# Cross-attention and feed-forward kernel on one core: the rounding of the last batch's main probabilities on ScalarE, and one part of a layer norm one slot later on POOL

## What is computed

```python
    x = x + _L0_xattn_ref(_layernorm(x), ctx_1024, ctx_1024, mask, w_q, w_k, w_v, w_o)
    x = x + _L0_ffn_ref(_layernorm(x), kernel, bias, a, b)
```

## Time and profile before

| what | value |
|---|---|
| runs of the kernel | 519.60, 517.91, 517.69 us; median 517.91 |
| the profiled execution | 519.61 us, its span 517.8 us |
| busy share of the span | PE 87%, DVE 80%, POOL 76%, ACT 63% |
| chain that ended last | PE 45%, DVE 28%, ACT 14%, POOL 6% |
| mean granted clock of TensorE | 0.96 of full speed |

### The profile page before, as it was taken

How to read it: one execution, slowest core, us unless ns; L and a number is a source line. 1 busy time by engine, 2 the same in 40 slices (tenths; PEclk the granted TensorE clock), 3 DMA queues, 4 the chain that set the end, 5 groups by cost and what they waited for, 6 DMA issues and landing times.

```text
span 517.8 us, 15453 instructions
## 1 busy us (share of the span) xinstructions
PE 448.1 (87%) x5855; PEld 328.1 (63%) x5855; DVE 412.6 (80%) x1122; ACT 324.6 (63%) x837; POOL 393.3 (76%) x652
## 2 busy tenths in 40 slices
PE   3219768999999999999999999999999999888873
PEld 0116246667866686677766786668666866666652
DVE  4955756888899897978898888989897978887662
ACT  4905446577667776677667766777677766665621
POOL 3356158798978897788879888889788887899941
PEclk9658979999999999999999999999999999999898
DMA  8320139767796699679967797669868886679950
GB/s 308 120 61 11 30 58 202 130 128 152 169 175 130 128 199 154 114 122 176 173 130 137 161 167 149 132 133 192 161 122 146 141 159 128 134 128 182 165 122 26
DMA packets 218817, 71.91 MB, mean 139 GB/s; under 512 B 202785, under 2 KB 216882, under 8 KB 218738
## 3 DMA queue, kind: packets, MB, share of 16 engines
q1 hardware_dynamic: 217680, 69.25, 69.6%
q0 software_dynamic: 480, 1.31, 1.1%
q10 hardware_dynamic: 578, 0.30, 0.2%
HBM read 14.71 MB, written 4.19 MB: 37 GB/s over the span
## 4 chain that ended last, share of the span: by engine, by line
PE 45%; DVE 28%; ACT 14%; POOL 6%; issue 3%; DMA 3%; POOLq 0%; DVEq 0%; ACTq 0%
PE ps_b L874 34%; ACT arena L646 8%; DVE ps_a L764 7%; PE ps_a L939 6%; DVE arena L757 4%; DVE arena L746 2%; ACT arena L637 2%; ACT arena L625 2%; PE ps_b L982 2%; PE ps_b L958 2%; DVE arena L712 2%; DVE arena L768 1%; DVE arena L837 1%; POOL arena L564 1%; POOL arena L560 1%
## 5 line engine op out<-in xcount | busy, mean ns | idle before, releaser
L874 PE MATMUL ps_b<-arena 128*128 128x65 f16 (+3 forms) x3384 | 328.8, 250 | 10.9 <-DVE arena L837 3.4
L874 PEld LDWEIGHTS ps_b<-arena 128*128 128x128 f16 x3384 | 226.8, 98 | 90.5 <-issue 5.9
L646 ACT ACTIVATE arena<-ps_a,arena 128x160 f32<-128x160 f32 x512 | 159.5, 394 | 95.8 <-DVE arena L768 88.5
L564 POOL TENSOR_TENSOR arena<-arena 128x512 f16<-128x512 f32 x128 | 148.1, 1157 | 0.0
L560 POOL CAST arena<-arena 128x512 f16<-128x512 f32 x128 | 78.1, 610 | 64.6 <-ACT arena L646 62.8
L764 DVE TENSOR_REDUCE ps_a<-ps_a 128x4 f32<-128x640 f32 x128 | 105.3, 822 | 0.0
L939 PE MATMUL ps_a<-arena 64*128 64x160 f16 x1536 | 76.8, 233 | 16.8 <-ACT arena L646 15.0
L939 PEld LDWEIGHTS ps_a<-arena 64*128 64x128 f16 x1536 | 51.2, 95 | 41.4 <-issue 23.8
L958 PE MATMUL ps_b<-arena 128*128 128x65 f16 x512 | 71.6, 194 | 0.0
L757 DVE TENSOR_TENSOR arena<-ps_b,arena 128x512 f16<-128x512 f32 x64 | 43.5, 686 | 24.5 <-ACT arena L637 23.7
L837 DVE TENSOR_TENSOR arena<-ps_b,arena 128x256 f32<-128x256 f32 x128 | 54.3, 424 | 4.4
(11 more groups left out here) (130 smaller groups left out, 401.5 us busy)
## 6 DMA issues: line engine op xcount, KB each, us to landing
arena<-in_x_dram SPq DMA_DIRECT2D x8, 512.0 KB, 5.2
mask_u<-in_x_dram SPq DMA_DIRECT2D x32, 128.0 KB, 3.1
out_dram<-mask_u SPq DMA_DIRECT2D x32, 128.0 KB, 2.8
arena<-arena SPq DMA_TRANSPOSE x128, 3.9
arena<-arena SPq DMA_DIRECT2D x24, 65.0 KB, 2.5
arena<-in_L_xattn_w_k_dram SPq DMA_DIRECT2D x1, 1024.0 KB, 8.1
arena<-in_L_xattn_w_v_dram SPq DMA_DIRECT2D x1, 1024.0 KB, 10.1
arena<-in_L_xattn_w_q_dram SPq DMA_DIRECT2D x1, 1024.0 KB, 11.9
```

What stands on the lines that cost most here:

```text
L564: nc.gpsimd.tensor_tensor(lo_main, main, hi_main, ALU.subtract)
L646: ins = nc.scalar.activation(probs[k % 2][:, h, :], p_scores[k % 2][:, h % 2, h // 2 * WINDOW:(h // 2 + 1) * WINDOW], ACT.Exp, bias=neg_ma ...
L874: mm = nc.tensor.matmul(dst, a, c, start=(first and at == 0), stop=(last and at == n - 1))
```

## The change

In slots 112 to 127 the high half of the main probabilities is made by ACT, right behind the four exponentials of the same slot, in place of POOL's L560. ACT's new instruction waits for the exponentials themselves and for the transpose of three slots before. POOL's low half of the main keys waits for ACT's new semaphore. Besides, the norm part that stood on POOL behind the split of slot 126 (it is tile 29's) stands behind the split of slot 127.

```diff
+        LATE_CAST = LAST - NS
...
-                nc.gpsimd.tensor_copy(hi_main, main).then_inc(p_hi_made, 1)
+                if k < LATE_CAST:
+                    nc.gpsimd.tensor_copy(hi_main, main).then_inc(p_hi_made, 1)
                 nc.gpsimd.tensor_copy(rests[:, :, 0:2, :], rest.unsqueeze(2).broadcast_to([P, GROUP, 2, REST])) \
                     .then_inc(p_hi_made, 1)
-                pool.wait_ge(p_hi_made, 2 * k + 1)
+                if k < LATE_CAST:
+                    pool.wait_ge(p_hi_made, 2 * k + 1)
+                else:
+                    pool.wait_ge(p_main_made, k - LATE_CAST + 1)
                 nc.gpsimd.tensor_tensor(lo_main, main, hi_main, ALU.subtract)
...
                 tile = s.k // NG - 2
-                if s.g == 2 and 0 <= tile < NT:
+                after_next = s.k == LAST - 2
+                if (s.g == 2 and not after_next or s.k == LAST - 1) and 0 <= tile < NT:
...
                 ins.then_inc(exp_made, 1)
+                if k >= LATE_CAST:
+                    old = k - HALF_BUFS
+                    act.wait_ge(turned[old % TURN_BUFS], 16 * (old // TURN_BUFS + 1))
+                    act.wait_ge(exp_made, k + 1)
+                    nc.scalar.activation(p_half[k % HALF_BUFS][:, 0], probs[k % 2][:, :, 0:P], ACT.Copy) \
+                        .then_inc(p_main_made, 1)
```

More of the change, by code:

```diff
@@ L300, in xattn_ffn @@
         p_hi_made = sem("p_hi_made")
+        p_main_made = sem("p_main_made")
         p_lo_made = sem("p_lo_made")
@@ L559, in split_probs @@
                 rests = rest_parts(k % HALF_BUFS)
-                nc.gpsimd.tensor_copy(hi_main, main).then_inc(p_hi_made, 1)
+                if k < LATE_CAST:
+                    nc.gpsimd.tensor_copy(hi_main, main).then_inc(p_hi_made, 1)
                 nc.gpsimd.tensor_copy(rests[:, :, 0:2, :], rest.unsqueeze(2).broadcast_to([P, GROUP, 2, REST])) \
                     .then_inc(p_hi_made, 1)
-                pool.wait_ge(p_hi_made, 2 * k + 1)
+                if k < LATE_CAST:
+                    pool.wait_ge(p_hi_made, 2 * k + 1)
+                else:
+                    pool.wait_ge(p_main_made, k - LATE_CAST + 1)
                 nc.gpsimd.tensor_tensor(lo_main, main, hi_main, ALU.subtract)
-                pool.wait_ge(p_hi_made, 2 * k + 2)
+                pool.wait_ge(p_hi_made, min(k + 1, LATE_CAST) + k + 1)
                 nc.gpsimd.tensor_tensor(rests[:, :, 2, :], rest, rests[:, :, 0, :], ALU.subtract).then_inc(p_lo_made, 1)
```

## The result

| | before | after |
|---|---|---|
| median of 20 runs each | 517.89 us | 518.79 us |
| lowest and highest | 517.10, 519.77 | 517.73, 521.43 |
| ratio of the runs | | 1.0022, 95% interval 1.0012 to 1.0032 |
| profiled execution, its span | 519.61, 517.8 us | 518.23, 516.4 us |

The account below looks back on a forecast made before the run. POOL was taken to bound the last batch's tiles, the next chain 0.83 us behind. Terms 0.65 - 0.6 + 0.1 - 1.7 - 1.5 + 0.4 = -2.65 took 519.61 to 517.0, adjusted to 516.8 us; range 515.8 to 519.0.

Parts of the forecast that it names:

- What bounds: Last batch: POOL fills its tiles; relieving it only uncovers the chain PE, DVE, ACT, PE, 0.83 us behind.
- Term 2: ACT's new rounding in each slot: takes 0.63 us and delays what follows on ACT by 0.65 us, bounds 0.5 and 0.9.
- Term 3: Entry, slot 112: the rounding stands ahead of v1, on which DVE and everything else wait; +0.65 us, once.
- Term 4: Tile periods: two tiles together -0.6 us, the first +0.1; ACT's waits for transposes 0, at most 0.4 a tile.
- one of the signs that the prediction named for being wrong: ACT's rounding in the last batch, L661, waiting for transposes would show the prediction wrong.
- Term 5: Last batch: PE's low clock, which cost 0.81 us in a period and 0.87 in w(29), does not recur there; -1.7 us.
- the clock falls again: Rival: PE's clock falls again somewhere between 480 and 500 us, the 1.7 us gain vanishes, 518.5 us; chance 0.15.
- The link from the profiled execution to the median: Of 1.7 us over the other runs, low clock explains 1.07; a third of the other 0.6 comes off, giving 516.8 us.
- Term 6: The end: the last split's transpose lands earlier, PE's 1.48 us of idling go, -1.5 us; late DVE adds +0.4.
- The rule of the Trainium skill: PE's clock falls back only behind an idle gap far longer than 1.35 us, so it would stay up in the tiles.

Follow-up runs that it names:

- e6: The change with extra PE matmuls in the last batch's pauses, twelve in slot 113 and five in the other tiles; median 516.45 us, ratio 0.9961.
- e3: The change with four buffers p_half in place of three, so a rounding waits for the transpose of k-4; median 518.68 us, ratio 1.0004.
- e1: The change with only the rounding on ACT, tile 29's norm part back behind the split of slot 126; median 520.05 us, ratio 1.0032.
- e9: The change with twelve extra PE matmuls in slot 113 alone, ahead of w(26); median 518.65 us, ratio 1.0001.
- e13: The kernel before with extra PE matmuls: 10 in each tile's pause, 4 ahead of w(30), 12 ahead of n(30); median 518.77 us, ratio 1.0019.
- e2: The kernel before with only tile 29's norm part moved, POOL rounding as before; median 519.93 us, ratio 1.0030.
- e8: The kernel before with tile 29's norm part moved and ten extra PE matmuls in each last-batch tile's pause; median 518.42 us, ratio 0.9974.
- e4: The change with the rounding on ACT from slot 113 on instead of 112; median 518.72 us, ratio 0.9999.
- e14: The change with extra PE matmuls: 12 in slot 113, 5 in other tiles, 4 ahead of w(30), 12 ahead of n(30); median 517.31 us, ratio 0.9989.
- e10: The change with rounding from slot 113, four buffers p_half, extra matmuls in tile pauses and ahead of n(30) and n(31); median 516.76 us, ratio 0.9966.

## Why the prediction was wrong

It had the size within 0.5% and the time within its range, and the sign wrong. From slot 112's exponentials on, its sum was -2.65 us, and the profiled executions differ by +0.15: from there to w(26) +1.03 (forecast +0.65; by e6 0.73, so the rest is low clock already), the three periods +0.48 (forecast -1.3), from w(29) to the end -1.36 (forecast -2.0). That the profiled execution of after is nevertheless 1.4 us the shorter of the two comes from ahead of slot 112, by chance and not by the change. By its own steps:

- **What bounds** held: POOL's loss of 0.55 us a slot gave 0.2 us a tile (11.03 to 10.85), because ACT's chain stood 0.83 us behind, as read from the earlier trace rows, and took most of that up itself.
- **Term 2**, the rounding: 0.63 us, as taken. The delay of what follows was 0.76, not 0.65: the two waits ahead of it leave 0.09 us after the exponentials' end, not 0.03. **Term 3**, the entry: 0.76 likewise.
- **Term 4**: 10.85 and 10.83 against the 10.8 forecast. The waits for transposes, put at nothing with 0.4 a tile as bound, were 1.11 and 0.67 us in two tiles, one of the signs that the prediction named for being wrong, and cost nothing there (e3, without them, has the same periods). At the last slot 1.28 us lay on the chain, and e3 puts its price at 0.45.
- **Term 5 is the step that failed**: "I expect it not to come again at this place: -1.7". At this place it didn't; it came at w(26) and cost 1.55 us from w(26) to w(27) (12.38 against e6's 10.83). By the runs' mean clocks it may have come more than once in eleven of the twenty, which are 1.8 us longer in the median. The pauses did get shorter in the later tiles (0.64 us where 1.35 was), which the prediction took for safety. The traces contradict that: in e1 and e9 the clock fell ahead of w(28), in a tile with no pause over 0.64 us, and in before it stayed full behind 1.62 and 1.54 us. The rival "the clock falls again" had 0.15 and a price of 518.5, and that is about what was measured (518.79), though the fall came near 454 us and not between 480 and 500. The price of the low clock was too high as well: in e13, with the clock full from w(26) up to w(30), the stretch is 1.2 us shorter than in before and not 1.7, since other waits take up the rest.
- **The link from the profiled execution to the median failed with it.** It put 1.07 of the 1.7 us between the runs down to the low clock in the last batch. But before's profiled execution was also late at slot 112: 448.68, the latest of the thirteen profiles of kernels that are alike up to there, whose median is 447.1. Those 1.5 us are nearly the whole excess over the median. Whether an ordinary run of before has the low clock in its last batch, one profile can't tell, so the -1.7 could not be counted against a median.
- **Term 6**: the idling of 1.48 us ahead of the values of 127 went, as said. But "ACT takes x2(29) only behind o1(30)" was wrong: x2 waited 0.88 us for the moved norm part, because the rounding of 127 waited 1.28 us for a transpose that took 5.17. From w(30) to w(31) the forecast's -1.1 came (7.02 for 8.11), but w(29) to w(30) took 8.98 where 9.34 less the low clock's 0.87 is 8.47, so half the gain went there. e2 shows the same place with 1.96 us of idling on PE.

The rule of the Trainium skill that the prediction names ("TensorE: Matmul & The Clock Gate", "Why this matters for your kernels") warns of long gaps between bursts of matmuls. The traces don't bear it out as a full account: ahead of w(26) in after, where the clock fell, the longest pause that the timeline shows was 1.62 us, and in e1, ahead of w(28), it was 0.64.

Shown: the part of the clock in the change, by e6 against it (0.9961 against 1.0022, intervals well apart, with only PE work added) and by the first period of the two traces. Without term 5 the sum is -0.95, and the traces at full clock come near that (an estimate from one trace each: 0.2 longer up to w(30), 1.1 shorter from there to w(31)). The mean clocks of the runs support it in the change and in e8, but not everywhere. In e2, e4 and e14 the longest runs have a mean of 0.986 to 0.988. In before, 33 runs at 0.958 have a median of 518.1 us and 16 at 0.960 one of 518.6, the wrong way round. Open: why the change's median suffers more from the clock than before's, whose tiles have longer pauses. Identical pauses ahead of w(26) brought the clock down in after and in e3 and not in e1. It may hang on where pauses lie to each other rather than on their length; no run here separates that.

## What to carry to other kernels

When an engine that sets the pace is relieved, the next chain stands close behind: read its waits for the first engine (here 0.83 us), not the first engine's busy time (8.8 us), as the gain. Where TensorE pauses in every round, as here by 0.4 to 1.6 us in some 11, look at its clock as a part of the schedule: it cost 1.55 us in one tile, more than the edit gave. Compare medians of many runs, look for the low stretch in more than one trace, and try cheap matmuls in the pauses before judging the edit. Before carrying a profiled execution's excess over the median to one stage, compare the starting times of one and the same instruction ahead of that stage in several traces.

## What the runs showed of the hardware

Adding matmuls made a kernel faster: e6 has 27 matmuls of 128 x 256 more than the change and is 0.6% faster. More of them isn't always better: with 12 and 20 of them added in the drain, e10's time outside its span grew by about 1 us. A low stretch costs what stands in it: w of 24 matmuls took 4.33 us instead of 2.78. DMA transposes of the same size landed 3.6 to 5.3 us after issue before and 3.6 to 5.6 after, with a median of 3.7 in both. Several of the long ones had a load or a store next to them in the queue; that this made them long wasn't tried. So a buffer wait that the median covers was not covered at three of the sixteen slots. Executions of kernels that are alike up to slot 112 reached it up to 2.3 us apart.
